# Gated recurrent cross attention on one core: log-distances that accumulate in their PSUM bank, and norm issued ahead of the output scale

## The chip, the cores and the metric

One core of a Trainium2 chip. Time is device time in microseconds (us) of one launch, the median of the runs shown; the program runs on one core only, so no other core takes part. The kernel is a whole two-layer decoder in one launch; the change lies in one of its stages, the cross attention of layer 0, which takes some 335 us of the 3032 us span.

## The reference, cut to what matters

For each of 32 batches (256 tokens, width 256) and 8 heads of width 32, with q the normalised x and k = v = the context:

```python
pre = 15 * tanh((concat(q, k, v) @ ifgate_w.T + ifgate_b) / 15)
i_pre, f_pre = split(pre)                     # one value per head and token each
lf = cumsum(log_sigmoid(f_pre))
log_d = lf[t] - lf[s] + i_pre[s]              # masked to -inf where s > t
m = max(log_d, over s)
d_mat = exp(log_d - m)
s_mat = (q_h @ k_h.T) / sqrt(32) * d_mat
h = (s_mat @ v_h) / (maximum(abs(sum(s_mat, over s)), exp(-m)) + 5e-5)
h = h * rsqrt(mean(h * h) + 1e-6) * (1 + outnorm_w)
x = x + h
```

## The kernel before

`layer0_mlstm` has two parts. `mlstm_gates` computes the pre-activations of all heads and also builds `minus`, a table of weights in bf16 [128, 4 lanes, 8 heads, 128]: for lane j (a batch's place in its group of four) and head h it holds -1 in the three rows that carry that head's running maximum (in three bf16 pieces), and 0 elsewhere. `mlstm_heads` does the attention proper.

In `mlstm_heads` the work goes by quads: q = 0 to 63, b = q // 2 the batch, c = q % 2 which four of its eight heads. S runs over 256 queries and two tiles of 128 keys, of which only three of four 128x128 blocks are needed, so that a head's tile is 128 x 384 (COLS). For head r of a quad:

- TensorE, `distances(q, r)` (L688, L689): into bank DD[r % 2] the product of `minus[:, j, h, :]` with `top3`, and on top of it the causal mask, identity times `maskneg`, 256 columns.
- ScalarE, `exp(q, r)` (L624, L625): decay = exp(bank + own term), in two pieces.
- TensorE, `scores(q)` (L700, L703): all four heads' key-query products, into four banks, once VectorE has done with the scores of the quad before.
- VectorE, `weigh(q)` (L804): sm = scores x decay, four instructions, one a head.
- TensorE, `values(q, n)` (L718, L722): outputs and denominators, transposed.

When a batch's two quads are done: ScalarE `gathered` copies outputs out of PSUM (L636, L637), TensorE `back` transposes them (L748) into the two DD banks, and ScalarE `back` copies these to `o[b % 2]` (L650), the buffer pair that holds the batch's un-normed output. Then VectorE `norm` (L810 to L822) computes the denominator, its reciprocal `rden` and the mean square `rms` (it needs GpSimd's `sq`, L595), ScalarE `root` turns `rms` into 1/sqrt, VectorE computes `scale` = rms x rden (L841), and GpSimd does y = o x scale (L599), yg = y x gain (L601), X += yg (L603). Last, VectorE takes the statistics of the new X rows for the next layer (L97, two bn_stats).

Every engine runs its own list in order, written out by hand; semaphores tie the lists. For a batch b (q = 2b and 2b + 1) they are:

- VectorE: weigh(2b), then weigh(2b + 1), [em], scale of batch b - 3, norm of batch b - 2, statistics of batch b - 4. Behind the products of quads 2, 3 and 4 of each group's eight, `prepare` adds the prefix work of the next group of four batches (parts 0, 1 and 2).
- ScalarE, even quad: exp of heads 0 and 1, copy L650 of batch b - 2, exp of heads 2 and 3, root of batch b - 3. The copy waits for the transposes and, `y_ready`, for y of batch b - 4, since it overwrites the `o` buffer that y reads.
- TensorE, even quad: scores(2b), transposes of batch b - 2, distances of heads 2 and 3 (they wait for the copy L650, which frees the banks), values of the quad before with distances 0 and 1 of the next quad between.
- GpSimd: sq(b), y(b - 1), yg, X, in this order for every b.

The names and lines: `distances` L677 to L689, `norm` L807 to L822, the loop of VectorE L826 to L845, `back` on ScalarE L645 to L650.

Of the kernel before, what the change touches and what calls it, by code (L numbers as in the profile page):

```python
# [6 lines left out]
ALU = mybir.AluOpType  # L7
# [4 lines left out]
P = 128  # L12
# [381 lines left out]
def mlstm_gates(nc, t, d, bank, s):  # L394

    ctx = ExitStack()
    with ctx:
# [2 lines left out]
        LANES = range(LANES4)  # L400
        gw, gc, bias, bias2 = sb("gw", [P, 6, 2, 32]), sb("gc", [P, DC, 2, 32]), sb("bias", [P, 2]), sb("bias2", [P, 2])
        low, high, heads, lane = sb("low", [P, 2 + 2 * HEADS]), sb("high", [P, 2 + 2 * HEADS]), sb("heads", [P, HEADS]), sb("lane", [P, LANES4])
        which = sb("which", [P, LANES4, HEADS])
        z = [sb(f"z{j}", [P, TB, D]) for j in LANES]
        qT = [[sb(f"qT{k}{j}", [P, DC, S]) for j in LANES] for k in range(2)]
        cT = [[sb(f"cT{k}{j}", [P, DC, S]) for j in LANES] for k in range(2)]
# [48 lines left out]
        def _(dve):  # L455
# [15 lines left out]
            for j in LANES:  # L471
                nc.vector.tensor_scalar(which[:, j, :], heads[:], lane[:, j:j + 1], -1.0, ALU.mult, ALU.mult).then_inc(rows_ready, 1)
            dve.wait_ge(rows_ready, 2 + LANES4)
            for g in range(GROUPS):
                for j in LANES:
                    tile = (g * LANES4 + j) * TB
                    if g:
                        dve.wait_ge(zT_raw, (g - 1) * LANES4 + j + 1)
                    for c in range(TB):
                        nc.vector.tensor_scalar(z[j][:, c, :], t["X"][:, tile + c, :], t["mean"][:, tile + c:tile + c + 1],  # L480
                                                t["rstd"][:, tile + c:tile + c + 1], ALU.subtract, ALU.mult).then_inc(z_ready, 1)
                if g < LANES4:
                    nc.vector.tensor_copy(s["minus"][:, g], which[:, g, :, None].to_broadcast([P, HEADS, P]))

        @block.tensor
        def _(pe):
# [57 lines left out]
def mlstm_heads(nc, t, d, bank, s):  # L544
    ctx = ExitStack()
    with ctx:
# [14 lines left out]
        oT = sb("oT", [P, 3, S])  # L561
        o = [sb(f"o{k}", [P, TB, COLS]) for k in range(2)]
        sq, y, yg = (sb(n, [P, TB, D]) for n in ("sq", "y", "yg"))
        den, neg, rden, rden2, ss, rms, scale = (sb(n, [P, TB, HEADS]) for n in ("den", "neg", "rden", "rden2", "ss", "rms", "scale"))
        names = ("soft0", "soft", "chain", "top3", "gT_raw", "gT", "mT", "em0", "em", "c_free", "dd", "decay", "sc", "sm", "pv", "oT", "bt", "o",
                 "sq", "small", "q_in", "rms_ln", "rms", "scale", "y", "yg", "x_done", "took_wait")
        (soft0, soft_ready, chain, top3_ready, gT_raw, gT_ready, mT_raw, em0, em_ready, c_free, dd_raw, decay_ready, sc_raw, sm_ready, pv_raw, oT_ready,
# [38 lines left out]
        def _(act):  # L606
# [44 lines left out]

            def root(b):
                act.wait_ge(q_in, b + 1)
                nc.scalar.activation(rms[:], rms[:], ACT.Ln, scale=1.0 / HD, bias=tiny[:]).then_inc(rms_ln, 1)
                act.wait_ge(rms_ln, b + 1)
                nc.scalar.activation(rms[:], rms[:], ACT.Exp, scale=-0.5).then_inc(rms_ready, 1)

            softplus(0)
            act.wait_ge(gT_raw, 1)
# [16 lines left out]
        def _(pe):  # L676
            def distances(q, r):  # L677
                b, c = q // 2, q % 2
                j, h, out = b % LANES4, QUAD * c + r, DD[r % 2]
                if r < 2:  # L680
                    if q:
                        pe.wait_ge(decay_ready, (q - 1) * QUAD + r + 3)
                elif not c and b > 1:
                    pe.wait_ge(o_ready, 2 * (b - 2) + r - 1)
                else:
                    pe.wait_ge(decay_ready, q * QUAD + r - 1)
                pe.wait_ge(top3_ready, b // LANES4 + 1)
# [82 lines left out]
        def _(dve):  # L770
# [35 lines left out]
            def norm(b):  # L806
# [5 lines left out]
                ch.did(nc.vector.tensor_tensor(den[:], den[:], neg[:], ALU.max)).see()  # L812
                dve.wait_ge(em_ready, g + 1)
                ch.did(nc.vector.tensor_tensor(den[:], den[:], em[g % 2][:, :, j, :], ALU.max)).see()
                ch.did(nc.vector.reciprocal(rden[:], den[:])).see()
                dve.wait_ge(sq_ready, b + 1)
                ch.did(nc.vector.tensor_reduce(ss[:], heads_of(sq[:]), AX.X, ALU.add))
                ch.did(nc.vector.tensor_tensor(rden2[:], rden[:], rden[:], ALU.mult)).see()
                ch.end()
                if b:  # L820
                    dve.wait_ge(scale_ready, b)
                nc.vector.tensor_tensor(rms[:], ss[:], rden2[:], ALU.mult).then_inc(q_in, 1)  # L822

            for part in range(3):
                prepare(0, part)
            for q in range(QUADS + 10):  # L826
# [1700 lines left out]
```

## Time and profile before

| | us |
|---|---|
| median of 3 runs | 3037.41 (3037.13 to 3038.9) |
| the profiled execution, its own time | 3033.9 |
| its span in the profile | 3031.8 |

Busy over the whole span: TensorE 2660.3 us (88%), VectorE 2117.7 (70%), ScalarE 1772.7 (58%), GpSimd 659.4 (22%). The stages follow one another with barriers between them, so a stage is read by itself; the heads stage lies between about 430 and 763 us. A timeline row gives the start, the length, the engine, the line and operation, output and inputs, the count of instructions merged in the row, and in brackets how long the engine was idle before it and what ended that.

### The profile page before, as it was taken

To read this page: it belongs to the slowest core of one execution; us is meant where nothing else is said; L and a number is where in the kernel's file an instruction comes from. 1 tells how busy PE (TensorE), PEld (TensorE's weight loads), DVE (VectorE), ACT (ScalarE), POOL (GpSimd) and SP (SyncE) were. 2 spreads that over 40 slices of the span, in tenths; PEclk is the share of its full clock that TensorE was granted. 3 is DMA by queue.
4 is the path that set the end of the run, shared out by engine and by line. 5 is a ranking of instruction groups with operands and counts; after the bars stand their busy time and mean duration, and the time that the engine had idled before them with its cause. 6 is when DMAs were issued, how large, how long until landed. Compare 5 with 4: busy or idle time off the path is not lost. (4 is left out here: it accounts for less than half of the span.)

```text
span 3031.8 us, 57744 instructions
## 1 busy us (share of the span) xinstructions
PE 2660.3 (88%) x20806; PEld 1987.7 (66%) x20807; DVE 2117.7 (70%) x3938; ACT 1772.7 (58%) x2891; POOL 659.4 (22%) x663
## 2 busy tenths in 40 slices
PE   8999889998796999999699999778999888567799
PEld 6777654444695888888577877645555555333587
DVE  5666648888343331111389999779999999867799
ACT  3333358777232222222266666479999999767786
POOL 0111103445375000100332321031222221200000
PEclk9999999999797999999899999889999999889899
DMA  4000162222676444444411110011111111034676
GB/s 133 1 1 1 31 229 85 75 85 64 242 264 216 142 144 144 141 142 142 138 46 41 37 41 22 4 41 26 27 28 29 30 29 29 3 153 194 221 230 202
DMA packets 135667, 291.85 MB, mean 96 GB/s; under 512 B 21520, under 2 KB 58384, under 8 KB 130832
## 3 DMA queue, kind: packets, MB, share of 16 engines
q1 hardware_dynamic: 117648, 237.39, 24.2%
q0 software_dynamic: 17792, 51.40, 5.2%
q8 instruction: 147, 2.41, 0.3%
q14 instruction: 80, 0.66, 0.1%
HBM read 184.90 MB, written 103.81 MB: 95 GB/s over the span
## 5 line engine op out<-in xcount | busy, mean ns | idle before, releaser
L1294 ACT ACTIVATE cx_h<-bank,c_b 128x256 f32<-128x256 f32 (+1 forms) x288 | 117.6, 459 | 388.4 <-PE bank L1246 388.4
L1951 DVE TENSOR_SCALAR e_low<-bank 128x2048 f32<-128x2048 f32 x128 | 293.3, 2291 | 28.4 <-PE bank L1844 28.4
L1246 PE MATMUL bank<-cx_zT,cx_w 128*128 128x256 f32 (+1 forms) x1152 | 250.1, 371 | 2.1 <-DMA cx_w<-cw_dram 1.2
L1826 ACT ACTIVATE e_low<-e_low 128x2048 f32<-128x2048 f32 x128 | 244.7, 1911 | 4.1
L1257 PE MATMUL bank<-c_w,cx_h 128*128 x1088 | 246.6, 379 | 0.0
L1824 ACT ACTIVATE e_low<-e_low 128x2048 f32<-128x2048 f32 x128 | 243.6, 1903 | 0.0
L1246 PEld LDWEIGHTS bank<-cx_zT,cx_w 128*128 128x128 f32 x1152 | 212.1, 192 | 30.3 <-DMA cx_w<-cw_dram 1.6
L1257 PEld LDWEIGHTS bank<-c_w,cx_h 128*128 128x128 f32 x1088 | 201.2, 190 | 24.4
L1844 PE MATMUL bank<-e_qT,e_kT 32*128 32x256 f32 x2048 | 147.2, 400 | 68.5 <-DVE e_high L1952 67.7
L1309 DVE COPY cx_zT<-bank 128x512 f32<-128x512 f32 (+1 forms) x72 | 47.7, 662 | 202.5 <-PE bank L1237 202.5
L1317 DVE TENSOR_TENSOR cx_y<-bank,c_b 128x512 f32<-128x512 f32 (+1 forms) x72 | 47.6, 661 | 199.0 <-PE bank L1257 199.0
L1469 POOL DMA_INDIRECT d_chosen<-slot_y,slot x128 | 130.0, 1016 | 240.5 <-DVE X L1680 208.2
L1844 PEld LDWEIGHTS bank<-e_qT,e_kT 32*128 32x128 f32 x2048 | 95.7, 184 | 125.7 <-issue 66.5
L1883 PE MATMUL bank<-e_high,e_vx 128*32 128x256 f32 x2048 | 160.9, 386 | 0.0
L804 DVE SCALAR_TENSOR_TENSOR b_sm<-bank,b_decay 128x384 f32<-128x384 f32 x256 | 129.4, 550 | 45.0 <-PE bank L703 30.5
L1883 PE MATMUL bank<-e_low,e_vx 128*32 128x256 f32 x2048 | 157.5, 379 | 0.0
L1952 DVE TENSOR_SCALAR e_high<-bank 128x1024 f32<-128x1024 f32 x128 | 155.3, 1213 | 0.0
L1823 ACT ACTIVATE e_high<-bank 128x1024 f32<-128x1024 f32 x128 | 131.1, 1025 | 38.2 <-DVE e_low L1951 32.0
L624 ACT ACTIVATE b_decay<-bank,b_gT 128x256 f32<-128x256 f32 x256 | 123.4, 482 | 40.2 <-PE bank L689 40.2
L1220 POOL DMA_DIRECT2D slot_y<-cx_y x64 | 45.8, 716 | 443.9 <-DVE cx_y L1317 435.7
L960 POOL DMA_INDIRECT expert_rows<-cr_z,cr_slot_row x128 | 124.1, 970 | 72.8 <-issue 37.8
L1802 POOL TENSOR_SCALAR e_z<-X,mean,rstd 128x256 f32<-128x256 f32 x64 | 77.7, 1224 | 270.6 <-PE bank L1854 270.6
(386 smaller groups left out, 6585.7 us busy)
## 6 DMA issues: line engine op xcount, KB each, us to landing
cx_w<-cw_dram SPq DMA_DIRECT2D x72, 512.0 KB, 3.6
hidden<-fu_h SPq DMA_DIRECT2D x32, 1024.0 KB, 3.8
fd_h<-hidden SPq DMA_DIRECT2D x64, 512.0 KB, 4.1
cx_rows<-expert_rows SPq DMA_DIRECT2D x64, 256.0 KB, 3.5
slot_y<-cx_y POOLq DMA_DIRECT2D x64, 256.0 KB, 2.6
g_cT<-ctxT_dram SPq DMA_DIRECT2D x32, 256.0 KB, 5.0
queries<-g_qT SPq DMA_DIRECT2D x32, 256.0 KB, 5.5
b_qT<-queries SPq DMA_DIRECT2D x32, 256.0 KB, 2.7
```

The source lines that it names most:

```text
L804: nc.vector.scalar_tensor_tensor(sm[q % 2][r][:], SC[r][:, 0:COLS], float(HD) ** -0.5, decay[r][:], ALU.mult, ALU.mult).then_inc(sm_ready, 1)
L960: pool.indirect_dma_start(s["rows"], bass.IndirectOffsetOnAxis(ap=slot_row[:, k, i * TT + n:i * TT + n + 1], axis=0), z[i % RING][:, n, :] ...
L1246: last = nc.tensor.matmul(H[k][f // 2][:, (f % 2) * GROUP_ROWS:(f % 2) * GROUP_ROWS + cols], w1[k][:, c, f * P:(f + 1) * P], zT[k][:, c, 0 ...
L1257: last = nc.tensor.matmul(Y[k][:, n * D:(n + 1) * D], h[k][:, f, n * P:(n + 1) * P], w2[:, bass.ds(e, 1), f, :].rearrange("p o d -> p (o d ...
L1469: pool.indirect_dma_start(chosen_y[b % RING][c][n][:], None, t["slot_y"], bass.IndirectOffsetOnAxis(ap=t["slot"][:, c, b * TB + n:b * TB + ...
L1823: nc.scalar.activation(flat(high[n % RING][:, 2:4]), t["psum"][:, 2:4, :].rearrange("p r s -> p (r s)"), ACT.Relu).then_inc(upper_ready, 1)
L1824: nc.scalar.activation(flat(low[n % RING][:]), flat(low[n % RING][:]), ACT.Ln, bias=1.0).then_inc(ln_ready, 1)
L1826: nc.scalar.activation(flat(low[n % RING][:]), flat(low[n % RING][:]), ACT.Exp, scale=-1.0).then_inc(low_ready, 1)
L1844: last = nc.tensor.matmul(bank[r][:, c2 * S:(c2 + 1) * S], kT[b % 2][rows_, e, c, c2 * P:(c2 + 1) * P], qT[b % 2][rows_, c, :], start=True ...
L1883: last = nc.tensor.matmul(U[quad][32 * r:32 * r + 32, 0:S], vx[b % 2][:, c2, 4 * quad + r, :], s[n % RING][:, r, c2, :], start=c2 + part = ...
L1951: nc.vector.tensor_scalar(flat(low[n % RING][:]), HEADS4.rearrange("p r s -> p (r s)"), -1.0, 0.0, ALU.mult, ALU.max).then_inc(neg_ready, 1)
L1952: nc.vector.tensor_scalar(flat(high[n % RING][:, 0:2]), HEADS4[:, 0:2, :].rearrange("p r s -> p (r s)"), 0.0, None, ALU.max).then_inc(high ...
```

## The change

Three things.

1. **Distances.** The table `minus` now holds, for lane j and head h, the weights that turn the distances of the head that used the same bank last into those of this head (new weights less the old ones): four small VectorE operations in `mlstm_gates` make `change` from `which`. `distances` issues a fresh product and the mask only where the bank was overwritten by the transposes (heads 2 and 3 of the first quad) or where a new group of four batches brings a new `top3` (heads 0 and 1 of lane 0). Elsewhere the product is added onto what lies in the bank (start=False), mask and all, and the mask matmul is dropped: it stays for 2.5 of 8 heads on average.
2. **VectorE's order.** In an odd quad norm of batch b - 2 comes first, the statistics of batch b - 4 next, and the scale of batch b - 3 last.
3. **Buffers.** `rden` and `rms` have two buffers each, since norm now writes them while the batch before still needs its own. Norm waits for the scale of two batches back, which is long done, and on its own step before.

```diff
@@ mlstm_gates, VectorE
+            nc.vector.tensor_copy(change[:, :, 2:4], which[:, :, 2:4]).then_inc(rows_ready, 1)
+            nc.vector.tensor_copy(change[:, 0, 0:2], which[:, 0, 0:2]).then_inc(rows_ready, 1)
+            nc.vector.tensor_tensor(change[:, :, 4:HEADS], which[:, :, 4:HEADS], which[:, :, 2:HEADS - 2], ALU.subtract).then_inc(rows_ready, 1)
+            nc.vector.tensor_tensor(change[:, 1:LANES4, 0:2], which[:, 1:LANES4, 0:2], which[:, 0:LANES4 - 1, HEADS - 2:HEADS], ALU.subtract).then_inc(rows_ready, 1)
+            dve.wait_ge(rows_ready, 6 + LANES4)
...
-                    nc.vector.tensor_copy(s["minus"][:, g], which[:, g, :, None].to_broadcast([P, HEADS, P]))
+                    nc.vector.tensor_copy(s["minus"][:, g], change[:, g, :, None].to_broadcast([P, HEADS, P]))
@@ distances(q, r), TensorE
-                nc.tensor.matmul(out[:, 0:COLS], minus[:, j, h, :], top3[b // LANES4 % 2][:], start=True, stop=False)
-                nc.tensor.matmul(wide(out), t["identb"][:], t["maskneg"][:].rearrange("p (x y) -> p x y", x=2), start=False, stop=True).then_inc(dd_raw, 1)
+                fresh = not c and (r > 1 or j == 0)
+                last = nc.tensor.matmul(out[:, 0:COLS], minus[:, j, h, :], top3[b // LANES4 % 2][:], start=fresh, stop=not fresh, skip_group_check=not fresh)
+                if fresh:
+                    last = nc.tensor.matmul(wide(out), t["identb"][:], t["maskneg"][:].rearrange("p (x y) -> p x y", x=2), start=False, stop=True)
+                last.then_inc(dd_raw, 1)
@@ norm(b), VectorE
-                ch.did(nc.vector.reciprocal(rden[:], den[:])).see()
+                if b > 1:
+                    dve.wait_ge(scale_ready, b - 1)
+                ch.did(nc.vector.reciprocal(rden[b % 2][:], den[:])).see()
                 dve.wait_ge(sq_ready, b + 1)
+                if b:
+                    dve.wait_ge(q_in, b)
                 ch.did(nc.vector.tensor_reduce(ss[:], heads_of(sq[:]), AX.X, ALU.add))
...
-                if b:
-                    dve.wait_ge(scale_ready, b)
-                nc.vector.tensor_tensor(rms[:], ss[:], rden2[:], ALU.mult).then_inc(q_in, 1)
+                nc.vector.tensor_tensor(rms[b % 2][:], ss[:], rden2[:], ALU.mult).then_inc(q_in, 1)
@@ VectorE's loop
-                if c and 0 <= b - 3 < B:
-                    dve.wait_ge(rms_ready, b - 2)
-                    if b > 3:
-                        dve.wait_ge(y_ready, b - 3)
-                    nc.vector.tensor_tensor(scale[:], rms[:], rden[:], ALU.mult).then_inc(scale_ready, 1)
                 if c and 0 <= b - 2 < B:
                     norm(b - 2)
                 if c and 0 <= b - 4 < B:
                     dve.wait_ge(x_done, b - 3)
                     update_stats(nc, t, (b - 4) * TB, took_wait)
+                if c and 0 <= b - 3 < B:
+                    dve.wait_ge(rms_ready, b - 2)
+                    if b > 3:
+                        dve.wait_ge(y_ready, b - 3)
+                    nc.vector.tensor_tensor(scale[:], rms[(b - 3) % 2][:], rden[(b - 3) % 2][:], ALU.mult).then_inc(scale_ready, 1)
```

VectorE, from one batch's four products of its second quad to the next batch's products, in a batch without prefix work. Before (L804 the products, L841 the scale, L810 to L822 norm, L97 the statistics):

```order
L841 TENSOR_TENSOR b_scale<-b_rms,b_rden 128x16
L810 TENSOR_SCALAR b_den<-b_o 128x16
L811 TENSOR_SCALAR b_neg<-b_o 128x16
L812 TENSOR_TENSOR b_den<-b_den,b_neg 128x16
L814 TENSOR_TENSOR b_den<-b_den,b_em 128x16
L815 RECIPROCAL b_rden<-b_den 128x16
L817 TENSOR_REDUCE b_ss<-b_sq 128x16
L818 TENSOR_TENSOR b_rden<-b_rden 128x16
L822 TENSOR_TENSOR b_rms<-b_ss,b_rden 128x16
L97 BN_STATS bn<-X 128x6 x2
L804 SCALAR_TENSOR_TENSOR b_sm<-bank,b_decay 128x384 x8
```

The same stretch of VectorE after (L814 the products, L858 the scale, L820 to L834 norm):

```order
L820 TENSOR_SCALAR b_den<-b_o 128x16
L821 TENSOR_SCALAR b_neg<-b_o 128x16
L822 TENSOR_TENSOR b_den<-b_den,b_neg 128x16
L824 TENSOR_TENSOR b_den<-b_den,b_em 128x16
L827 RECIPROCAL b_rden<-b_den 128x16
L831 TENSOR_REDUCE b_ss<-b_sq 128x16
L832 TENSOR_TENSOR b_rden<-b_rden 128x16
L834 TENSOR_TENSOR b_rms<-b_ss,b_rden 128x16
L97 BN_STATS bn<-X 128x6 x2
L858 TENSOR_TENSOR b_scale<-b_rms,b_rden 128x16
L814 SCALAR_TENSOR_TENSOR b_sm<-bank,b_decay 128x384 x8
```

The scale has moved from ahead of eight operations of norm and two of statistics to behind them; nothing else of VectorE's list moved.

TensorE, from the transposes of a batch's outputs (L748) to the next quad's second distances, behind which a mask (L689) and the scores (L700) follow, before:

```order
L748 MATMUL bank<-ident,b_oT 128x128 x6
L688 MATMUL bank<-b_top,b_minus 128x384
L689 MATMUL bank<-maskneg,identb 128x2x128
L688 MATMUL bank<-b_top,b_minus 128x384
L689 MATMUL bank<-maskneg,identb 128x2x128
L718 MATMUL bank<-b_sm,b_cn 32x256 x4
L722 MATMUL bank<-b_sm,b_pick 32x256 x4
L688 MATMUL bank<-b_top,b_minus 128x384
L689 MATMUL bank<-maskneg,identb 128x2x128
L718 MATMUL bank<-b_sm,b_cn 32x128 x4
L722 MATMUL bank<-b_sm,b_pick 32x128 x4
L688 MATMUL bank<-b_top,b_minus 128x384
```

The same stretch of TensorE after, to the scores (L710):

```order
L758 MATMUL bank<-ident,b_oT 128x128 x6
L696 MATMUL bank<-b_top,b_minus 128x384
L698 MATMUL bank<-maskneg,identb 128x2x128
L696 MATMUL bank<-b_top,b_minus 128x384
L698 MATMUL bank<-maskneg,identb 128x2x128
L728 MATMUL bank<-b_sm,b_cn 32x256 x4
L732 MATMUL bank<-b_sm,b_pick 32x256 x4
L696 MATMUL bank<-b_top,b_minus 128x384
L728 MATMUL bank<-b_sm,b_cn 32x128 x4
L732 MATMUL bank<-b_sm,b_pick 32x128 x4
L696 MATMUL bank<-b_top,b_minus 128x384
L710 MATMUL bank<-b_qT,b_cT 128x256 x4
```

The two masks right behind the transposes are still there; those of the next quad's heads 0 and 1 are gone.

## Rows read from the trace of the kernel before

**Rows 1.** Busy time by engine in the steady part: PE, PEld, DVE, ACT, POOL, clock, DMA.

```profile
472.00:745.00 273.00, 250.28 (x3350) 136.01 (x3347) 233.50 (x614) 216.68 (x641) 130.54 (x113) 1.00 0.25 80
```

**Rows 2.** Waits, 446 to 735 us: us in total, times, longest us.

```profile
POOL b_y L599 <- DVE b_scale L841: 134.2, 27, 6.2
...
ACT b_o L650 <- POOL b_y L599: 5.6, 5, 1.3
```

**Rows 3.** Timeline of two cycles: start us, us, engine, line, operation, idle before.

```profile
571.87 0.17 DVE L841 TENSOR_TENSOR b_scale<-b_rms,b_rden 128x16 f32<-128x16 f32 x1
...
572.11 1.05 POOL L599 TENSOR_TENSOR b_y<-b_o,b_scale 128x512 f32<-128x512 f32 x1 [6.00 <-DVE b_scale L841]
...
573.19 0.87 ACT L650 ACTIVATE b_o<-bank 128x384 f32<-128x384 f32 x2 [1.05 <-POOL b_y L599]
...
581.00 0.16 DVE L841 TENSOR_TENSOR b_scale<-b_rms,b_rden 128x16 f32<-128x16 f32 x1
...
581.37 0.95 DVE L812 TENSOR_TENSOR b_den<-b_den,b_neg 128x16 f32<-128x16 f32 x1
...
582.10 0.88 PE L748 MATMUL bank<-ident,b_oT 128*128 128x128 f32 x6
...
582.74 0.87 ACT L650 ACTIVATE b_o<-bank 128x384 f32<-128x384 f32 x2 [0.68 <-PE bank L748]
...
584.52 1.93 DVE L804 SCALAR_TENSOR_TENSOR b_sm<-bank,b_decay 128x384 f32<-128x384 f32 x4
...
586.44 0.27 PE L689 MATMUL bank<-maskneg,identb 128*128 128x256 bf16 x1
...
586.64 0.71 PE L700 MATMUL bank<-b_qT,b_cT 32*128 32x256 f32 x8
...
590.18 0.17 DVE L841 TENSOR_TENSOR b_scale<-b_rms,b_rden 128x16 f32<-128x16 f32 x1
```

**Rows 4.** Timeline, earlier copies and scales, the first copy a late one.

```profile
543.87 0.87 ACT L650 ACTIVATE b_o<-bank 128x384 f32<-128x384 f32 x2 [2.15 <-PE bank L748]
...
545.73 1.18 DVE L804 SCALAR_TENSOR_TENSOR b_sm<-bank,b_decay 128x384 f32<-128x384 f32 x2 [0.56 <-ACT b_decay L625]
...
551.30 0.16 DVE L841 TENSOR_TENSOR b_scale<-b_rms,b_rden 128x16 f32<-128x16 f32 x1
...
553.64 0.87 ACT L650 ACTIVATE b_o<-bank 128x384 f32<-128x384 f32 x2 [0.84 <-PE bank L748]
...
561.05 0.17 DVE L841 TENSOR_TENSOR b_scale<-b_rms,b_rden 128x16 f32<-128x16 f32 x1
...
563.21 0.87 ACT L650 ACTIVATE b_o<-bank 128x384 f32<-128x384 f32 x2 [0.67 <-PE bank L748]
```

**Rows 5.** Timeline, the maximum in norm while GpSimd is idle.

```profile
462.47 0.18 DVE L812 TENSOR_TENSOR b_den<-b_den,b_neg 128x16 f32<-128x16 f32 x1
```

**Rows 6.** Timeline, prefix work, the products behind it, and GpSimd's square.

```profile
566.43 0.68 DVE L779 TENSOR_TENSOR_SCAN b_cum<-b_one,b_soft 128x256 f32<-128x256 f32 x1
...
568.67 2.06 DVE L804 SCALAR_TENSOR_TENSOR b_sm<-bank,b_decay 128x384 f32<-128x384 f32 x4
...
575.88 1.04 POOL L595 TENSOR_TENSOR b_sq<-b_o 128x512 f32<-128x512 f32 x1
...
577.24 0.41 DVE L790 TENSOR_TENSOR b_lo<-b_rest,b_mid 128x256 bf16<-128x256 f32 x1
...
579.14 1.94 DVE L804 SCALAR_TENSOR_TENSOR b_sm<-bank,b_decay 128x384 f32<-128x384 f32 x4
```

**Rows 7.** The scale's line (count, durations in ns, first and last start), then the tail.

```profile
L841 DVE TENSOR_TENSOR b_scale<-b_rms,b_rden x32: 161/165/543, 472.2 to 757.6; 128x16 f32<-128x16 f32 x32
...
744.50 0.17 DVE L841 TENSOR_TENSOR b_scale<-b_rms,b_rden 128x16 f32<-128x16 f32 x1
...
748.58 1.02 DVE L811 TENSOR_SCALAR b_neg<-b_o 128x16 f32<-128x16 f32 x1
...
760.65 1.26 POOL L603 TENSOR_TENSOR X<-b_yg,X 128x512 f32<-128x512 f32 x1
```

More of the change, by code:

```diff
@@ L402, in mlstm_gates @@
         low, high, heads, lane = sb("low", [P, 2 + 2 * HEADS]), sb("high", [P, 2 + 2 * HEADS]), sb("heads", [P, HEADS]), sb("lane", [P, LANES4])
-        which = sb("which", [P, LANES4, HEADS])
+        which, change = sb("which", [P, LANES4, HEADS]), sb("change", [P, LANES4, HEADS])
         z = [sb(f"z{j}", [P, TB, D]) for j in LANES]
@@ L563, in mlstm_heads @@
         sq, y, yg = (sb(n, [P, TB, D]) for n in ("sq", "y", "yg"))
-        den, neg, rden, rden2, ss, rms, scale = (sb(n, [P, TB, HEADS]) for n in ("den", "neg", "rden", "rden2", "ss", "rms", "scale"))
+        den, neg, rden2, ss, scale = (sb(n, [P, TB, HEADS]) for n in ("den", "neg", "rden2", "ss", "scale"))
+        rden, rms = ([sb(f"{n}{k}", [P, TB, HEADS]) for k in range(2)] for n in ("rden", "rms"))
         names = ("soft0", "soft", "chain", "top3", "gT_raw", "gT", "mT", "em0", "em", "c_free", "dd", "decay", "sc", "sm", "pv", "oT", "bt", "o",
@@ L653, in root @@
                 act.wait_ge(q_in, b + 1)
-                nc.scalar.activation(rms[:], rms[:], ACT.Ln, scale=1.0 / HD, bias=tiny[:]).then_inc(rms_ln, 1)
+                own = rms[b % 2][:]
+                nc.scalar.activation(own, own, ACT.Ln, scale=1.0 / HD, bias=tiny[:]).then_inc(rms_ln, 1)
                 act.wait_ge(rms_ln, b + 1)
-                nc.scalar.activation(rms[:], rms[:], ACT.Exp, scale=-0.5).then_inc(rms_ready, 1)
+                nc.scalar.activation(own, own, ACT.Exp, scale=-0.5).then_inc(rms_ready, 1)
             softplus(0)
@@ L814, in norm @@
                 ch.did(nc.vector.tensor_tensor(den[:], den[:], em[g % 2][:, :, j, :], ALU.max)).see()
-                ch.did(nc.vector.reciprocal(rden[:], den[:])).see()
+                if b > 1:
+                    dve.wait_ge(scale_ready, b - 1)
+                ch.did(nc.vector.reciprocal(rden[b % 2][:], den[:])).see()
                 dve.wait_ge(sq_ready, b + 1)
+                if b:
+                    dve.wait_ge(q_in, b)
                 ch.did(nc.vector.tensor_reduce(ss[:], heads_of(sq[:]), AX.X, ALU.add))
-                ch.did(nc.vector.tensor_tensor(rden2[:], rden[:], rden[:], ALU.mult)).see()
+                ch.did(nc.vector.tensor_tensor(rden2[:], rden[b % 2][:], rden[b % 2][:], ALU.mult)).see()
                 ch.end()
-                if b:
-                    dve.wait_ge(scale_ready, b)
-                nc.vector.tensor_tensor(rms[:], ss[:], rden2[:], ALU.mult).then_inc(q_in, 1)
+                nc.vector.tensor_tensor(rms[b % 2][:], ss[:], rden2[:], ALU.mult).then_inc(q_in, 1)
             for part in range(3):
```

## The prediction

> **What bounds the kernel now.** I read three views. The busy time over 472 to 745 us shows the heads stage in its steady part: TensorE 250 of 273 us, VectorE 234, ScalarE 217, clock fully granted [rows 1]. So at first sight TensorE is the bound and cheaper matmuls pay. The list of waits adds two lines that matter more: GpSimd waits 134 us for `scale`, and ScalarE's copy of the outputs (L650) has already waited for GpSimd's `y` five times [rows 2]. The timeline then shows the loop that closes through them.
>
> I call S the moment when VectorE starts its first small operation behind the four products of a batch's second quad, and K the start of ScalarE's copy L650 for the batch before. Before, the first small operation is `scale`. With q the quad and b = q // 2, the order around K is: `scale(b-4)` on VectorE, `y(b-4)` on GpSimd, which reads the same `o` buffer that L650 for batch b-2 overwrites, so L650 waits for it; L650 frees the two distance banks, so TensorE's distances of quad q, head 2 wait for it, and everything queued behind them on TensorE: `values(q-1)`, the distances of q+1, `scores(q+1)`, hence VectorE's next products and the next S. Read it in [rows 3]: S 571.87, `y` 572.11 to 573.16, K 573.19, with the wait put down to L599. One cycle on, S is 581.00 and TensorE's transposes L748 run from 582.10 to 582.98; the copy starts at 582.74 with the first transposed half. There `y`, done at S+1.3, was out of the way by about half a microsecond; where VectorE was late it had no slack at all.
>
> Four consecutive cycles [rows 3, 4]: S to K 2.34 (551.30 to 553.64), 2.16, 1.32, 1.74, sum 7.56; K to next S 7.41, 8.66, 7.81, 7.44, sum 31.32. Together 38.9 us for four batches. The four differ because prefix work (`prepare`) falls on two of them. One cycle tells whether K to S has slack: at 543.87 the copy came late, ScalarE having sat idle for 2.15 us, and the next S is at 551.30, 7.43 later, as in the other cycle of its kind (7.44) [rows 3, 4]. So nothing is recovered: what delays K delays the next S in full. The clock stayed at full grant over this whole stretch [rows 1].
>
> **The moved scale (the term that decides).** After the change VectorE does norm, then the two bn_stats, then `scale`. Before, S to the next products took 3.52 us (581.00 to 584.52), with `scale` in front. Of this, L812 took 0.95 us although it has 16 elements a partition; with GpSimd idle it took 0.18 [rows 3, 5]. It started while `y` ran and ended with it (581.37 + 0.95 = 582.32, and 581.00 + 0.24 + 1.05 = 582.29 for `y`). In the new order GpSimd is idle during norm, so 0.77 goes, and 0.1 more in L818. What stands ahead of `scale` is 3.52 - 0.77 - 0.08 (its own slot) - 0.08 = 2.6 us. Then 0.24 to the start of `y`, 1.05 for `y`, 0.03 to K: 3.9, and 0.05 for two added satisfied waits: S to K = 3.95 in every cycle, 15.8 for four, against 7.56. VectorE's 0.8 us are real but not on this path: its products of quad q, heads 2 and 3 must wait for K anyway.
>
> **The removed masks.** 5.5 of 8 heads lose the 256-column matmul: 176 of 256. Start to start it holds the queue 0.20 (586.44 to 586.64 [rows 3]), part of which is the dispatch of the next waits; half of it, 0.11, is my lower value. At one batch that is 0.6 to 1.1 us of TensorE, but only two masks lie between K and S (quad q+1, heads 0 and 1; heads 2 and 3 of q keep theirs, since the transposes have overwritten the bank). I take 0.11 each, 0.22 a cycle, where TensorE is last, and nothing where ScalarE is (the cycle with the softplus). TensorE would then idle about 2.5 us in each cycle, between the end of the transposes (S+2.0) and the copy's first half (K+0.55 = S+4.5).
>
> **Prefix work meets GpSimd.** GpSimd's `sq` starts 3.77 behind the start of `y` (572.11 to 575.88 [rows 3, 6]), so at K+2.7 in the new order, to K+3.7. The products of quad q then end at K+3.04 (the late cycle: 545.73+1.18 against 543.87 [rows 4]), and `prepare` part 0 (566.43 to 568.67, 2.24 us) or part 2 (577.24 to 579.14, 1.9 us) starts there, with operations of two SBUF inputs (L779, L790) [rows 6]. Before, part 2 started 0.3 behind the end of `sq` (577.24 against 576.92). Bounds: not held at all, 0; held till `sq` ends, 0.7 each. The nearest rows, L812 in steady state and L811 held 1.02 us under `sq` in the tail [rows 3, 7], say held; I take that. Then K to S becomes, cycle by cycle: with parts 0 and 1, 3.75 + 2.24 + 2.0 for the four products + 1.2 for part 1 and `em` (from the products of 568.67, done at 570.7, to S 571.87) = 9.2, before 8.66; with part 2, 3.75 + 1.9 + 2.0 = 7.6, before 7.81; the plain one 7.44 - 0.22 = 7.2; the one in which ScalarE has the softplus 7.4, as before. Sum 31.4. Without the hold the first two are 8.5 and 7.1 (there ScalarE's exponentials end the cycle), sum 30.2.
> The Trainium skill, "SBUF — State Buffer", section "SBUF: two separate sides", says the same in a rule: a VectorE instruction with two SBUF inputs and a GpSimd instruction that reads SBUF exclude each other, whoever is first keeps the port for its whole instruction. By that rule, the L812 row agrees (0.95 against 0.18), the sum is the higher of the two below; if it didn't reach the scan L779, the lower.
>
> **The sum.** New group of four 15.8 + 31.4 = 47.2 us. From the fourth batch's S (472.2) to the last full one (744.50) there are 28 cycles in 272.3 us [rows 7]; now 7 x 47.2 = 330.4: +58.1. Without the hold, 7 x 46.0 = 322: +49.7.
> Tail: before, GpSimd runs y, yg, X, sq back to back, 4.8 a batch, from 744.50 to 761.9 (760.65+1.26) [rows 7]. Now `scale` also waits for norm, which waits for `sq`, and for the statistics: first `scale` 2.6 later, then GpSimd idle about 2 us in each of two more batches and 1.4 in the last: +8.
> Head of the stage: three batches without `y` in the loop, fewer masks: -2. Four small operations ahead of the gates' loop at up to the 0.18 of a small operation [rows 5], overlapping: +0.5.
> Total +64.6 (without the hold +56). Against the profiled execution, 3033.9 (its span 3031.8 and 2.1 around it, which stays): 3098.5. The median shown is 3.5 above it: 3102.
>
> **Rivals.**
> 1. The clock falls in the new 2.5 us gap. For: no stretch of the steady part has a gap of that length in every cycle. Against: around the late copy TensorE also stood, and the granted clock is 1.00 for the whole steady part [rows 1, 4]. Part of the stream behind each gap (K+0.55 to the scores at K+3.4, 2.9 us) at 1.2 instead of 2.4 GHz would add up to 2.9; at 1.5 a cycle 42 us: 3144.
> 2. Half recovered: with the whole loop slower, the other engines run further ahead, and K to S falls to about 6.5 in all four, 26 a group. Then 7 x 41.8 = 293: +20, with tail +27: 3064. Against: 7.43 in the late cycle.
> 3. Faster: `y` stays off the loop. It would be so if the copy waited for an older `y` than I read, or if `y` ended by S+1.8, when the transposes are through; it decides at that point, and 3.95 is 2.1 us past it. Then S to K stays, 0.22 comes off K, the statistics' cycle 0.8 of VectorE, together 0.7 a batch: 28 x 0.7 = 20 off: 3017.
> 4. Accumulating onto the old bank does not shorten the queue (the mask's slot was filled by waits): 28 x 0.22 = 6 on top of the forecast, 3108, inside its range.
>
> **Chances.** A measurement of this kernel tells about 0.2% (6 us) from no change. Forecast 0.83, rival 1 0.06, rival 2 0.05, rival 3 0.05, and 0.01 for within 0.2%. So faster 0.05, same 0.01, slower 0.94. Range of the forecast alone: no hold and 0.2 a mask gives 3088; waits costing 0.1 more in each cycle and a held `y` or `X` 3112. Stretched towards rivals 1 and 2: 3078 to 3122.
>
> **What the new profile would show.** L650 waits for GpSimd's `y` in nearly every batch, some 2 us each, where before it was TensorE's transposes; S to K near 3.95; the norm's maximum (L812 before) at 0.18; GpSimd's idle ahead of `y` still large; TensorE busy near 70% of the steady part, clock 1.00; cycles near 11.8 us instead of 9.7. I would be wrong if L650 still waits for TensorE, or if K to S is far from 7.4.

## The result, and the profile after

| | before | after |
|---|---|---|
| median of 3 runs, us | 3037.41 (3037.13 to 3038.9) | 3111.45 (3109.18 to 3112.51) |
| span of the profiled execution, us | 3031.8 | 3109.7 |
| attention stage, from the last statistics of one stage to those of the next, us | 399.6 | 473.3 |

The ratio is 1.0242, 95% interval 1.0222 to 1.0262: the changed kernel is 2.4% slower. Of the 77.9 us that the span gained, 73.7 lie in the attention stage, 0.9 ahead of it and 3.3 behind it, where both kernels are the same. The attention stage of the table is the gates and the heads together; the heads alone are the 335 us named at the start. In the changed kernel L820 to L834 are norm, L858 the scale, L814 the products, L656 ScalarE's copy of the outputs, L696 and L698 distances and mask, L758 the transposes, L605, L607, L609 and L601 GpSimd's `y`, `yg`, `X` and `sq`. S is now the start of L820, K that of L656.

Busy time of the steady part (the columns as in [rows 1]: start:end, length, busy us and instructions of PE, PEld, DVE, ACT, POOL, then granted clock, DMA share, GB/s):
```profile
472.00:745.00 273.00, 205.96 (x2564) 109.00 (x2560) 183.35 (x501) 173.94 (x519) 100.87 (x88) 0.92 0.21 68
```
TensorE is busy 75% of the stretch where it was 92%, and the granted clock of 0.92, not 1.00, says that something beside the wait happened. The waits of the same stretch (total us, times, longest), which answer to [rows 2]:
```profile
POOL b_y L605 <- DVE b_scale L858: 162.9, 22, 9.1
ACT b_o L656 <- POOL b_y L605: 63.1, 22, 4.3
PEld bank L696 <- ACT b_o L656: 62.6, 44, 3.9
```
The copy waited five times for `y` before, 5.6 us in all; now it does so in every batch of the window, 2.9 us each on average. One cycle, from S to the held prefix work behind K, answers to [rows 3] (rows of the timeline; "[3.84 <-POOL b_y L605]" is the idle time ahead and what ended it):
```profile
596.47 0.17 DVE L820 TENSOR_SCALAR b_den<-b_o 128x16 f32<-128x16 f32 x1
596.57 0.88 PE L758 MATMUL bank<-ident,b_oT 128*128 128x128 f32 x6
...
596.76 0.17 DVE L822 TENSOR_TENSOR b_den<-b_den,b_neg 128x16 f32<-128x16 f32 x1
...
598.39 0.75 DVE L97 BATCH_NORM_STATS2 bn<-X 128x6 f32<-128x256 f32 x2
599.06 0.16 DVE L858 TENSOR_TENSOR b_scale<-b_rms,b_rden 128x16 f32<-128x16 f32 x1
599.13 1.01 DVE L814 SCALAR_TENSOR_TENSOR b_sm<-bank,b_decay 128x384 f32<-128x384 f32 x2
599.30 1.05 POOL L605 TENSOR_TENSOR b_y<-b_o,b_scale 128x512 f32<-128x512 f32 x1 [9.10 <-DVE b_scale L858]
600.38 0.87 ACT L656 ACTIVATE b_o<-bank 128x384 f32<-128x384 f32 x2 [3.84 <-POOL b_y L605]
...
600.92 0.34 PE L696 MATMUL bank<-b_top,b_minus 128*128 128x384 bf16 x1 [3.48 <-ACT b_o L656]
...
602.79 1.08 PE L732 MATMUL bank<-b_sm,b_pick 128*32 128x256 f32 x8
...
603.00 1.04 POOL L601 TENSOR_TENSOR b_sq<-b_o 128x512 f32<-128x512 f32 x1
603.35 0.97 DVE L800 TENSOR_TENSOR b_lo<-b_rest,b_mid 128x256 bf16<-128x256 f32 x1
...
608.73 0.17 DVE L820 TENSOR_SCALAR b_den<-b_o 128x16 f32<-128x16 f32 x1
```
S to K is 600.38 - 596.47 = 3.91. The chain is scale 599.06, `y` 599.30, copy 600.38, distances 600.92; TensorE has nothing from the end of the transposes at 597.45. The maximum L822 takes 0.17, since GpSimd is idle beside it. K to the next S is 8.35. The matmuls show why it isn't 7.3: the eight L732 take 1.08 here and 0.61 to 0.64 elsewhere. The granted clock, us by us:
```profile
600.00:601.00 1.00, 0.08 (x1) 0.08 (x2) 0.15 (x1) 0.62 (x2) 0.92 (x2) 1.00 0.00 0
601.00:602.00 1.00, 1.00 (x8) 0.22 (x12) 0.00 (x0) 0.84 (x3) 0.92 (x2) 0.68 0.00 0
602.00:603.00 1.00, 1.00 (x13) 0.53 (x16) 0.69 (x2) 0.97 (x5) 1.00 (x1) 0.50 0.00 0
603.00:604.00 1.00, 1.00 (x12) 0.10 (x1) 1.00 (x2) 0.21 (x1) 1.00 (x2) 0.50 0.07 16
604.00:605.00 1.00, 1.00 (x17) 0.58 (x16) 0.96 (x3) 0.66 (x2) 0.04 (x1) 0.61 0.00 0
605.00:606.00 1.00, 1.00 (x22) 0.76 (x17) 0.85 (x3) 0.65 (x3) 0.00 (x0) 1.00 0.00 0
```
Shortly after TensorE resumes it runs at 0.50, the lower level (1.2 GHz), for about 3 us, and is back at full speed by 605.

From the fourth batch's S (474.81) to the last full one (811.18) the 28 cycles take 336.4 us, against 272.3 [rows 7]. S to K is 3.89 to 3.91 in 27 of them and 3.21 in the first. K to S differs: the cycle with prefix parts 0 and 1 takes 8.84 to 9.94, the one with part 2 7.29 to 8.36, the plain one 7.21 to 8.73, the one with the softplus 7.40, once 8.16; the last three, without prefix work, 6.83 to 7.32. The granted clock sorts them: in 14 of the 28 cycles it is 1.00 from end to end, and there K to S is 8.84, 7.29, 7.21 and 7.40 by kind; in the other 14 it is 0.86 to 0.88 over the cycle, and they take 0.7 to 1.5 us more than their kind, 15.1 us together.

### The profile page after: what moved, and what is told of

The parts are those of the page before. It is cut to its first block and busy times, and to the rows that moved or that the text cites. A ratio compares the mean times of both kernels' runs of the same rounds, so it can differ in the third digit from the quotient of the medians.

```text
span 3109.7 us, 57395 instructions
## 1 busy us (share of the span) xinstructions
PE 2670.7 (86%) x20630; PEld 1989.8 (64%) x20631; DVE 2106.6 (68%) x3942; ACT 1770.4 (57%) x2891; POOL 657.4 (21%) x663
## 5 line engine op out<-in xcount | busy, mean ns | idle before, releaser
L814 DVE SCALAR_TENSOR_TENSOR b_sm<-bank,b_decay 128x384 f32<-128x384 f32 x256 | 135.9, 554 | 121.0 <-ACT b_decay L631 73.3
L696 PE MATMUL bank<-b_top,b_minus 128*128 128x384 bf16 x256 | 86.3, 354 | 71.2 <-ACT b_o L656 64.9
```

The lines of the kernel that those rows point to most:

```text
L814: nc.vector.scalar_tensor_tensor(sm[q % 2][r][:], SC[r][:, 0:COLS], float(HD) ** -0.5, decay[r][:], ALU.mult, ALU.mult).then_inc(sm_ready, 1)
```

## The experiments

There are eleven runs with a trace, in three groups, each group on one chip with its own runs of the kernel before beside it. The kernel before took 3109.93 us beside the first group (e_order, e_mask, e_stats_last, e_o3), 3038.11 and 3037.08 beside the other two; the difference is in the two stages behind this one (1273 to 1280 us in the first group, 1200 to 1203 otherwise), and the attention stage is not touched by it. So runs are compared as ratios to before within a group, and by the attention stage's own time.

**e_order: the new order and buffers alone.** The masks and the fresh products stay:
```diff
-                    nc.vector.tensor_copy(s["minus"][:, g], change[:, g, :, None].to_broadcast([P, HEADS, P]))
+                    nc.vector.tensor_copy(s["minus"][:, g], which[:, g, :, None].to_broadcast([P, HEADS, P]))
...
-                fresh = not c and (r > 1 or j == 0)
+                fresh = True
```


> Only the order and the double buffers of the change, masks and old table kept. If the late scale is the cause, nearly all of the loss stays: the changed kernel's 3111 plus the two masks that lie on each cycle's chain, 28 x 0.2 to 0.4, so 3115 to 3122; S to K 3.9 us in every cycle. If accumulating in the bank (the other part) had cost the time, this kernel would be at or below 3037. The copy L656's wait should be put down to GpSimd's y in all steady batches.

Measured: 3190.43 against 3109.93, ratio 1.0267 (1.0238 to 1.0297); attention stage 480.1; S to K 3.90. That is the ratio I expected (3115 to 3122 of 3037 is 1.026 to 1.028). The whole loss, and a little more, comes with the order.

**e_mask: the dropped masks alone**, in the kernel before, with its order and single buffers:
```diff
-                nc.tensor.matmul(out[:, 0:COLS], minus[:, j, h, :], top3[b // LANES4 % 2][:], start=True, stop=False)
-                nc.tensor.matmul(wide(out), t["identb"][:], t["maskneg"][:].rearrange("p (x y) -> p x y", x=2), start=False, stop=True).then_inc(dd_raw, 1)
+                fresh = not c and (r > 1 or j == 0)
+                last = nc.tensor.matmul(out[:, 0:COLS], minus[:, j, h, :], top3[b // LANES4 % 2][:], start=fresh, stop=not fresh, skip_group_check=not fresh)
+                if fresh:
+                    last = nc.tensor.matmul(wide(out), t["identb"][:], t["maskneg"][:].rearrange("p (x y) -> p x y", x=2), start=False, stop=True)
+                last.then_inc(dd_raw, 1)
```


> Only the accumulation and the dropped masks, in the old order of VectorE. If the late scale is the cause, this part alone is a gain: 5.5 masks of 0.11 to 0.20 us come off TensorE a batch, VectorE then bounds near 9.2 a batch instead of 9.7, so 3037 less 28 x 0.3 to 0.6: 3020 to 3029. If accumulation costs as much as the mask did, 3037. If accumulation is behind the loss, above 3060.

Measured: ratio 0.9991 (0.9976 to 1.0005), attention stage 399.9: a miss, less than I expected (3020 to 3029 of 3037 is a ratio of 0.994 to 0.997). Its four cycles are 9.57, 10.69, 9.14 and 8.95, those before 9.58, 10.82, 9.13 and 9.18: only the plain cycle, in which TensorE is last, gains what the masks took (0.23). VectorE or ScalarE ends the others. The 28 cycles give 269.0 against 272.3. And in this execution the start of the stage gives it back: the fourth batch's scale starts 112.6 us into the stage, before 109.0. The granted clock (third column from the right) near the start of the stage, in e_mask:
```profile
440.00:442.00 2.00, 1.60 (x5) 0.41 (x3) 1.51 (x3) 1.40 (x5) 0.00 (x0) 0.50 0.00 0
442.00:444.00 2.00, 1.83 (x17) 1.29 (x17) 0.56 (x1) 1.92 (x6) 0.00 (x0) 0.50 0.00 0
444.00:446.00 2.00, 2.00 (x22) 0.69 (x22) 1.39 (x3) 1.20 (x4) 0.00 (x0) 0.50 0.00 0
```
The kernel before has 1.00 in the same three windows. But e_mask2 below, the same kernel once more, has 1.00 from 442 on and its fourth scale at 110.9, so the dropped masks are not shown to be what keeps the clock low there.

**e_stats_last: the scale one step earlier.** From the changed kernel, VectorE does norm, the scale, and the statistics last:
```diff
                 if c and 0 <= b - 2 < B:
                     norm(b - 2)
-                if c and 0 <= b - 4 < B:
-                    dve.wait_ge(x_done, b - 3)
-                    update_stats(nc, t, (b - 4) * TB, took_wait)
                 if c and 0 <= b - 3 < B:
...
+                if c and 0 <= b - 4 < B:
+                    dve.wait_ge(x_done, b - 3)
+                    update_stats(nc, t, (b - 4) * TB, took_wait)
```


> The changed kernel with scale between norm and the statistics instead of behind them. If the copy waits for y in every cycle, S to K shortens by just the two bn_stats, 0.67 (3.9 to 3.2), in 28 cycles, 19 us, plus 3 in the tail, plus up to 7 if the shorter TensorE gap keeps the clock up: 3082 to 3092. If only some cycles are bound by y the gain is under 10 us.

Measured: ratio 1.0131 (1.0099 to 1.0162), attention stage 438.9, 34 us below the changed kernel's 473.3, a little more than expected. Its S to K is 3.21 to 3.22 in every cycle:
```profile
562.86 1.05 POOL L605 TENSOR_TENSOR b_y<-b_o,b_scale 128x512 f32<-128x512 f32 x1 [5.68 <-DVE b_scale L855]
563.94 0.87 ACT L656 ACTIVATE b_o<-bank 128x384 f32<-128x384 f32 x2 [1.72 <-POOL b_y L605]
...
564.48 0.34 PE L696 MATMUL bank<-b_top,b_minus 128*128 128x384 bf16 x1 [1.36 <-ACT b_o L656]
```
The 0.68 that the scale is earlier arrives in full in 27 of the 28 cycles (18.5 us; the first had 3.21 before as well). The cycles give 28.1 in all (336.4 - 308.3), and the other 9.6 lie in K to S: the slow clock is gone from the plain cycle and the one with parts 0 and 1 (7.21 and 8.85 in all six groups), and is left in the one with part 2, where TensorE's gap is 2.85 to 3.00 long (8.18 to 8.35). In cycles of one kind at full clock K to S is the same in both kernels within 0.02 us while S to K is 0.68 shorter: S to K is paid one for one.

**e_o3: the copy freed from `y`.** From the changed kernel, three `o` buffers, so that the copy waits for the `y` of a batch earlier:
```diff
-        o = [sb(f"o{k}", [P, TB, COLS]) for k in range(2)]
+        o = [sb(f"o{k}", [P, TB, COLS]) for k in range(3)]
...
-                if b > 1:
-                    act.wait_ge(y_ready, b - 1)
+                if b > 2:
+                    act.wait_ge(y_ready, b - 2)
```


> The changed kernel with three output buffers instead of two: the copy of batch b waits for the y of b - 3, so the late scale has a whole batch more. Work, order and everything else as changed. If the loop scale, y, copy, distances is the cause, all of the loss goes and the removed masks and the shorter norm show: cycle 8.7 to 9.2 us, tail 5 to 8 us longer than before, total 3010 to 3030. If the loss came from the clock by itself or from the port shared with GpSimd, it would stay above 3080.

Measured: ratio 1.0091 (1.0061 to 1.0121), attention stage 426.9. No copy waits for `y` any more and S to K is 0.5 to 2.5 in most cycles (before 1.3 to 2.3). So 46 of the stage's 74 us go with this one wait, the slow clock behind TensorE's gaps among them: it is 0.98 here from 472 to 760. I expected all of it back, and that is a miss: 27 remain. The cycles of a group are mostly 12.02, 10.53, 8.95 and 9.57 to 9.86; the first two, with the prefix work, are 1.2 and 1.4 (against 10.82 and 9.13 before) too long. GpSimd's row and VectorE's in the second of them:
```profile
581.29 1.05 POOL L605 TENSOR_TENSOR b_y<-b_o,b_scale 128x512 f32<-128x512 f32 x1 [6.82 <-DVE b_scale L858]
582.42 1.27 POOL L607 TENSOR_TENSOR b_yg<-b_y,b_gain 128x512 f32<-128x512 f32 x1
583.77 1.33 POOL L609 TENSOR_TENSOR X<-b_yg,X 128x512 f32<-128x512 f32 x1
585.07 1.09 POOL L601 TENSOR_TENSOR b_sq<-b_o 128x512 f32<-128x512 f32 x1
```
```profile
582.99 0.98 DVE L800 TENSOR_TENSOR b_lo<-b_rest,b_mid 128x256 bf16<-128x256 f32 x1
583.89 1.36 DVE L801 TENSOR_SCALAR b_y<-b_hi,b_part 128x256 f32<-128x256 bf16 x1
585.29 1.15 DVE L802 SCALAR_TENSOR_TENSOR b_y<-b_mid,b_part,b_y 128x256 f32<-128x256 bf16 x1
586.47 0.48 DVE L805 SCALAR_TENSOR_TENSOR b_top<-b_lo,b_part,b_y 128x256 bf16<-128x256 bf16 x1
```
Each of the three VectorE operations ends 0.15 to 0.3 us after a GpSimd operation ends (583.97 after 583.69, 585.25 after 585.10, 586.44 after 586.16). With GpSimd idle they take 0.34 (L801) and 0.48 (L802), read in the changed kernel at 604.24 and 604.62. The Trainium skill, "SBUF — State Buffer", section "SBUF: two separate sides", calls the shared port an exclusive lock that whoever starts first keeps for its whole instruction; these rows agree, and in them GpSimd goes straight on to its next instruction.

VectorE is busy through this whole cycle, so the holds can be added up. L800, L801 and L802 take 2.26 us more than unheld; norm's L812 and L818, held before (0.96 and 0.24), take 0.18 and 0.17 now, 0.85 less. The difference is 1.41, and the cycle is 1.40 longer than before.

**e_o3_thin: is it that port?** From e_o3, `yg` and `X` work on 16 of 256 columns, so that the gain and the residual sum of the other 240 are left out (the stages behind then work on other data, and only the attention stage is read):
```diff
-                    nc.gpsimd.tensor_tensor(yg[:], y[:], gain[:, None, :].to_broadcast([P, TB, D]), ALU.mult).then_inc(yg_ready, 1)
+                    nc.gpsimd.tensor_tensor(yg[:, :, 0:16], y[:, :, 0:16], gain[:, None, 0:16].to_broadcast([P, TB, 16]), ALU.mult).then_inc(yg_ready, 1)
...
-                    nc.gpsimd.tensor_tensor(x, yg[:], x, ALU.add).then_inc(x_done, 1)
+                    nc.gpsimd.tensor_tensor(x[:, :, 0:16], yg[:, :, 0:16], x[:, :, 0:16], ALU.add).then_inc(x_done, 1)
```


> The kernel with three o buffers (e_o3), and GpSimd's gain product (L607) and residual add (L609) done on 16 of the 256 columns, so that the gain and the residual sum of the other 240 are left out; y and sq stay whole. Theory A: what is left of e_o3's loss in the attention stage (426.9 against 399.6 us) is VectorE's prefix work lengthened beside y, gain product, X and sq on GpSimd (L800 0.98, L801 1.36, L802 1.15 us there, against 0.41, 0.34 and 0.48). Then with two of the four gone, the cycles that hold that work come down from 12.0 and 10.5 us to 9.9 to 10.7 and 8.5 to 9.2, and the stage to 405 to 412. Rival B: the cycles are long because of the order alone (the ready norm work stands before the prefix work and the products of the next block): then the durations of L800 to L802 fall but the stage stays at 420 to 427.

Measured: 3037.04 in one run, before 3037.08; attention stage 400.0, even below what theory A gave. The two cycles are 10.72 and 9.15, those before 10.82 and 9.13. The same place:
```profile
575.81 1.05 POOL L605 TENSOR_TENSOR b_y<-b_o,b_scale 128x512 f32<-128x512 f32 x1 [8.01 <-DVE b_scale L858]
576.94 0.25 POOL L607 TENSOR_TENSOR b_yg<-b_y,b_gain 128x32 f32<-128x32 f32 x1
577.27 0.25 POOL L609 TENSOR_TENSOR X<-b_yg,X 128x32 f32<-128x32 f32 x1
577.48 1.04 POOL L601 TENSOR_TENSOR b_sq<-b_o 128x512 f32<-128x512 f32 x1
```
```profile
577.51 1.29 DVE L800 TENSOR_TENSOR b_lo<-b_rest,b_mid 128x256 bf16<-128x256 f32 x1
578.72 0.34 DVE L801 TENSOR_SCALAR b_y<-b_hi,b_part 128x256 f32<-128x256 bf16 x1
579.10 0.48 DVE L802 SCALAR_TENSOR_TENSOR b_y<-b_mid,b_part,b_y 128x256 f32<-128x256 bf16 x1
```
L801 and L802 are at 0.34 and 0.48 again, and only L800 is held, by `sq`: 0.88 of hold where e_o3 had 2.26, and the cycle is shorter by the same 1.38. The order is the same as in e_o3, so rival B has fallen. Of e_o3's 27 us the 28 cycles account for 18.7 (291.0 against 272.3) and the tail, where GpSimd's list sets the pace, for 7.4. The thin kernel has 270.7 and no longer tail; but there its shorter GpSimd list alone would also shorten the tail, so only the cycles' part is shown to be the port: of the 18.7, the 16.2 in the twelve cycles with prefix work. The other 2.5 are not explained.

**e_mid: the scale where nothing should be held.** Back at single buffers and dropped masks, with the scale inside norm, behind the maximum that the trace before shows held (0.95, [rows 3]):
```diff
-                ch.did(nc.vector.tensor_tensor(den[:], den[:], neg[:], ALU.max)).see()
+                ch.did(nc.vector.tensor_tensor(den[:], den[:], neg[:], ALU.max))
+                if b:
+                    scaled(b - 1)
+                ch.see()
```


> Masks dropped as in the change, but scale issued inside norm, just behind the maximum, with single buffers. The maximum then runs with GpSimd idle (0.18 instead of 0.95), y starts 0.5 later than before (S + 0.75), so that K comes at S + 1.8, as early as the transposes allow. The two cycles of four in which VectorE is last, those with prefix work, gain up to 0.77 each, the others nothing: attention stage 5 to 12 us under the kernel before, and with the masks' 3 a total 5 to 14 us faster, ratio 0.995 to 0.9985. If VectorE is not last in those cycles, no gain over the mask part alone (0.999). If the later GpSimd work now holds the prefix work, the cycles with it get longer and it is slower.

Measured: ratio 0.9998 (0.9989 to 1.0007), attention stage 400.4: a miss. The maximum (L826) is short, but the hold has moved to another operation with two SBUF inputs:
```profile
561.32 0.17 DVE L826 TENSOR_TENSOR b_den<-b_den,b_neg 128x16 f32<-128x16 f32 x1
...
561.66 1.05 POOL L604 TENSOR_TENSOR b_y<-b_o,b_scale 128x512 f32<-128x512 f32 x1 [4.82 <-DVE b_scale L818]
562.78 1.27 POOL L606 TENSOR_TENSOR b_yg<-b_y,b_gain 128x512 f32<-128x512 f32 x1
562.83 1.26 DVE L839 TENSOR_TENSOR b_rms<-b_ss,b_rden 128x16 f32<-128x16 f32 x1
```
L839 takes 1.26 for 16 elements a partition, beside `yg` (and 1.25 or 1.26 in nearly every batch); with GpSimd idle 0.17 (L834 in the changed kernel).

**e_mask_o3 and e_mask2: is e_mask held back by `y`?** e_mask with the third buffer of e_o3 (the same two edits), and e_mask once more on the same chip:

> The dropped mask products alone in the old order (e_mask), and three o buffers. Theory A: in the old order the copy of o waits on y only where y is the last thing to come (5 times of 28 at b_o in the kernel before, 5.6 us in all), and VectorE bounds those cycles anyway; then the ratio is 0.994 to 0.999, within 3 us of e_mask's. Rival B: y's wait is what kept e_mask from its gain: then the four cycles 9.6, 10.7, 9.1, 9.0 lose about 1 us in each of the first two, 14 us in all, and the ratio is 0.993 to 0.995.

> The dropped mask products alone (e_mask again, on the same chip as e_mask_o3): ratio 0.997 to 0.9995, attention stage 398 to 400.5 us. It only tells whether the 0.1% seen before repeats.

Measured: e_mask_o3 0.9998 (0.9989 to 1.0007), attention stage 398.4; e_mask2 0.9988 (0.9979 to 0.9997), stage 398.7. Freed from `y`, the kernel is no faster than with it, so rival B has fallen (its ratio is even above the range I gave). e_mask2 repeats the 0.1%. It is the only version whose interval lies below 1 (its gain is then 1 to 6 us); the first e_mask's interval, to 1.0005, doesn't exclude none. No version ran clearly ahead of the kernel before.

**e_before2, e_after2 and e_fill: what the clock costs.** Both kernels unchanged, and the changed one with 18 matmuls of zeros added onto `O` behind the transposes, so that TensorE works through its gap:
```diff
                     last.then_inc(bt_raw, 1)
+                for _ in range(18):
+                    nc.tensor.matmul(O[:, 0:S], t["identb"][:], zero[:].bitcast(BF)[:, 0:S], start=False, stop=True, skip_group_check=True)
```


> The kernel before, for its trace on the chip of these runs. The attention stage (row statistics to row statistics) 399 to 401 us, as in the trace before; whatever else differs in the span lies in the expert and time-mix stages, 1273 to 1280 against 1202.

> The changed kernel, for its ratio and trace on the chip of these runs. Late scale: attention stage 473 us again, 74 more than before, so a ratio of 1.022 to 1.026 at any level of the other stages.

> The changed kernel with 18 matmuls of 256 columns of zeros, about 1.9 us, behind the transposes, in the gap where TensorE waits for the copy; they add zero to a finished output region, so nothing else changes. If the slower clock in the cycles behind the long gaps is what makes K to the next S 8.2 to 8.7 in them instead of 7.2 to 7.3, these cycles come down, about 0.3 a cycle on average: attention stage 8 to 12 us shorter than the changed kernel's. If the clock costs nothing there, no change; if the filler runs into the copy's end, a few us longer.

Measured: e_before2 3034.86 with a stage of 398.8; e_after2 ratio 1.0236 (1.022 to 1.0253), stage 475.9, 77.1 above e_before2's; e_fill 1.0208 (1.0192 to 1.0224), stage 464.4. In e_fill the copy still waits for `y` in all 28 cycles, and the clock stays up in 26 of them. A gap filled, and 40 us of the stage; then one of the two cycles in which the clock fell all the same:
```profile
562.53 2.13 PE L761 MATMUL bank<-b_zero,identb 128*128 128x256 bf16 x18
564.90 0.34 PE L696 MATMUL bank<-b_top,b_minus 128*128 128x384 bf16 x1 [0.24 <-ACT b_o L656]
```
```profile
555.00:595.00 40.00, 36.67 (x486) 22.03 (x482) 28.32 (x74) 28.73 (x88) 15.60 (x14) 1.00 0.24 81
...
501.84:514.10 12.26, 10.15 (x113) 5.69 (x113) 9.06 (x25) 6.40 (x19) 4.58 (x4) 0.86 0.21 64
```
K to S is 8.84, 7.28, 7.21 and 7.40 by kind in most cycles; six of the 28 are longer, two with the low clock (by 1.1 and 0.8) and four at full clock (by 2.0 together; in three of these TensorE waits 0.9 to 1.0 us for the DMA into `b_cn` ahead of the scores). The 28 take 325.2 us (478.05 to 803.3 on norm's first line), 11.1 less than the changed kernel's 336.4 and 15.7 less than e_after2's 340.9, in which the clock fell in 18 cycles. More useless work on TensorE made the kernel 9.7 us faster in the medians (3111.44 to 3101.74).

## Why the prediction held, and where it was off

The forecast of 3102 was 9.5 us below the measured 3111.45, inside the range of 3078 to 3122; slower, as forecast.

- **S to K.** Forecast 3.95, measured 3.90 in nearly every cycle; the copy waits for `y` and not for the transposes, 2.9 us each where I wrote some 2. The maximum at 0.17 against a forecast 0.18. e_stats_last and e_o3 show the mechanism on both sides: less delay of the scale comes back one for one, and without the wait the 3.9 is gone.
- **K to next S.** Forecast 9.2, 7.6, 7.2 and 7.4, sum 31.4. At full clock it is 8.84, 7.28, 7.21 and 7.40 (e_fill, and the changed kernel's own cycles within 0.01), sum 30.7: between my two ends, with and without the hold (31.4 and 30.2). The prefix work is held by 0.57 each and not by 0.7, in nearly every group of e_fill: the scan (L791 there) takes 1.25 and not 0.68, the subtraction (L802 there, L800 in the changed kernel) 0.98 and not 0.41. Group of four 46.3 against a forecast 47.2. The 28 cycles less the 15.1 us of slow clock are 321.3, +49.0 against my +58.1. Of the 9.1 too much, 2.1 are S to K, 4.1 the twelve cycles with prefix work, and 3.0 the last three cycles, to which I gave prefix work that they don't have.
```profile
589.73 1.25 DVE L791 TENSOR_TENSOR_SCAN b_cum<-b_one,b_soft 128x256 f32<-128x256 f32 x1
```
- **The clock: the term that was mis-sized.** I gave it nothing in the sum, and 0.06 as rival 1 at 42 us. It was neither: it falls in 14 of the 28 cycles and costs 0.7 to 1.5 us there, 15.1 us in the profiled execution, a third of rival 1's price. e_fill, which kept it up in 26, took back 11.1 net of its own longer cycles. So the granted clock of 1.00 that I named as a sign failed (0.92), and TensorE is busy 75% where I wrote near 70%. My reason against it was the late copy of [rows 4], one gap with a clock of 1.00 over the window; a single gap did not speak for one in every cycle. With it, +49.0 + 15.1 = +64.1 for the 28 cycles.
- **Masks.** 0.22 in the plain cycle, where TensorE is last: 0.23 measured in e_mask; there the other three gained 0.13, 0.01 and nothing, and I had counted nothing for them.
- **Tail.** Forecast +8: from the last S (811.18) to the last statistics it is 26.2, before 18.3: +7.9.
- **Head of the stage and gates.** Forecast -2 + 0.5 = -1.5, measured +1.7 (S of the fourth batch at 474.81 against 472.18, less the 0.9 ahead of the stage). Between e_before2 and e_after2 the same difference is +0.2, so most of the +1.7 is not steady from one execution to the next; its cause stays open, and the gain of 2 that I forecast is in neither pair.
- **Ahead of and behind the stage.** +0.9 and +3.3, forecast 0. The code is the same; single runs of the kernel before on one chip lie between 3031.8 and 3041.74, so I take no cause from it.

Sum: 64.1 + 7.9 + 1.7 + 0.9 + 3.3 = 77.9, the span's growth, against +64.6 forecast. The direction and the wait were reasoned; that the total came within 10 us is in part luck: 9.1 too much in the cycles stood against 15.1 of slow clock counted as nothing. The medians differ by 74.0, since the profiled execution of before was 3.5 below its median.

Rival 2 (half recovered) and rival 3 (`y` off the loop) fell: K to S stayed at 7.2 or more as long as there was prefix work, and S to K was under 3.89 in the first cycle alone. What I had not seen is that taking the wait away isn't enough: e_o3 keeps 27 us of loss, because the order also brings GpSimd's four operations behind the products, beside the prefix work, and VectorE's operations are held there (2.26 us in the cycle shown). Before, the same four operations ran beside norm, where they cost VectorE 0.85 a batch, most of it in the row [rows 3] that had looked like the waste.

## What to carry to other kernels

When an operation of a few elements hands work to another engine, ask what waits for that engine's result two steps on (a buffer that it reads and another overwrites) before moving it back in its list: here the 0.68 us of the statistics came back as 0.68 us a batch, while the work put ahead of the scale gained nothing. An operation that is held by GpSimd shows where the port is taken. Moving what starts GpSimd moved the hold here: in e_mid to the next product with two SBUF inputs, in the new order to the prefix work. Only the kernel with less GpSimd work beside VectorE's (e_o3_thin) had less of it. Where a change opens a gap in TensorE's stream in every cycle, price the clock for what follows the gap too, even where one such gap passed unharmed.

## What the runs showed of the hardware

- The clock did not follow the gap's length alone: behind gaps of 3.48 and 3.49 the next S came after 8.35 in one cycle and 7.29 in the other of the same kind, and behind 1.76 after 8.56 where 2.12 gave 7.21 (the rows and the 4 us behind each; the clock is the third column from the right). In the cycle at 596.47 it was 1.00 in the gap and in the microsecond in which TensorE started again, and lower in the four after it.
```profile
514.68 0.34 PE L696 MATMUL bank<-b_top,b_minus 128*128 128x384 bf16 x1 [1.76 <-ACT b_o L656]
613.18 0.34 PE L696 MATMUL bank<-b_top,b_minus 128*128 128x384 bf16 x1 [2.12 <-ACT b_o L656]
...
515.10:519.10 4.00, 4.00 (x39) 1.61 (x38) 1.12 (x2) 2.50 (x8) 2.62 (x3) 0.62 0.00 0
613.60:617.60 4.00, 4.00 (x57) 2.06 (x56) 1.40 (x3) 3.57 (x12) 2.62 (x3) 1.00 0.14 34
```
- With matmuls of zeros in the gap (18 of 256 columns, 2.13 us) the granted clock was 1.00 in 26 of the 28 cycles, without them in 14 (in e_after2 in 10).
- A VectorE operation with one SBUF tensor as input and a column of scalars was held by GpSimd as well: L801 took 1.36 and not 0.34.
- The same kernel took 3109.93 us beside the first group of runs and 3038.11 and 3037.08 beside the other two, 2.4% apart and nearly all of it in the two stages behind this one, by the traces of the other kernels in each group. The first and the third group ran on a chip of the same number at different times, so it isn't the chip alone; the cause is open. Times compared over two groups would have been off by as much as the effect studied here.
